# Feed-forward part over two rows at once, with the residual's scaling on ScalarE and the gate on VectorE

## What is computed

```
u  = layernorm(x)                               # over the 256 channels
xh, z = split(u @ W_in)                         # 512 + 512 channels
xc = depthwise conv 3x3 of xh
dt_r, B, C = split(xc @ W_xproj);  dt = softplus(dt_r @ W_dt + b_dt)
h_t = exp(dt_t * A) * h_(t-1) + (dt_t @ W_dtN + b_dtN) * B_t * xc_t      # over 48*48 steps, 512 x 16 states
y_t = sum over states of h_t * C_t + Dskip * xc_t
y  = (layernorm(y) * ln_g + ln_b) * silu(z)     # the gate
x  = x + y @ W_out + b_out                      # the residual
n  = layernorm(x)
out = x + n + two one-hot vectors of 16, times 2 where a token is marked   # "ffn"
```

## Time and profile before

| | us |
|---|---|
| median of 3 runs | 3854.43 (3844.46 to 3861.37) |
| the profiled execution | 3850.34, of which the span from first to last instruction 3848.5 |
| VectorE busy | 3545.4 (92% of the span) |
| POOL, TensorE, ScalarE busy | 3123.7 (81%), 3007.7 (78%), 2946.9 (77%) |
| mean granted TensorE clock | 0.858 of full speed |
| DMA engines | 78.4% of their time, 205 GB/s |

### The profile page before, as it was taken

How to read it: one execution, slowest core, us unless ns; L and a number is a source line. 1 busy time by engine, 2 the same in 40 slices (tenths; PEclk the granted TensorE clock), 3 DMA queues, 4 the chain that set the end, 5 groups by cost and what they waited for, 6 DMA issues and landing times.

```text
span 3848.5 us, 105654 instructions
## 1 busy us (share of the span) xinstructions
PE 3007.7 (78%) x34944; PEld 1624.3 (42%) x34944; DVE 3545.4 (92%) x12174; ACT 2946.9 (77%) x6050; POOL 3123.7 (81%) x5772
## 2 busy tenths in 40 slices
PE   4787888788778887888788878877887788778765
PEld 2344444444444444444444444444444444444332
DVE  2699999999999999999999999999999999999997
ACT  2678777887787778787888787778887888787764
POOL 0688888888888888888888888888888888888885
PEclk7788888888888998888799888988888889988877
DMA  2878887887788878887888778778887888788874
GB/s 60 214 196 216 223 212 201 215 226 205 206 214 220 210 209 211 216 215 209 210 223 215 207 209 223 207 205 208 221 218 205 214 212 222 205 213 217 211 189 105
DMA packets 397438, 790.44 MB, mean 205 GB/s; under 512 B 94553, under 2 KB 249178, under 8 KB 396890
## 3 DMA queue, kind: packets, MB, share of 16 engines
q1 hardware_dynamic: 396890, 783.68, 78.4%
HBM read 648.20 MB, written 96.73 MB: 194 GB/s over the span
## 4 chain that ended last, share of the span: by engine, by line
DVE 43%; ACT 22%; PE 17%; issue 8%; DMA 3%; POOL 3%; SPq 2%; ACTq 0%; POOLq 0%; DVEq 0%
DVE h L910 9%; DVE ps_a L894 7%; ACT ps_a L668 7%; DVE ps_a L897 6%; DVE h L913 6%; PE ps_s L615 4%; PE ps_y L510 3%; ACT ap L678 3%; PE ps_s L577 3%; DVE sz L966 2%; DVE res L1001 2%; ACT y L753 2%; ACT yn L803 2%; PE ps_y L494 2%; ACT xtok L703 2%
## 5 line engine op out<-in xcount | busy, mean ns | idle before, releaser
L668 ACT ACTIVATE ps_a<-dtb,a_n 128x384 f32<-128x384 f32 x2304 | 1252.8, 580 | 387.5 <-DVE h L913 375.7
L1181 POOL TENSOR_TENSOR h<-mp,up 128x128 f32<-128x128 f32 x2304 | 1056.6, 459 | 392.3 <-PE ps_y L510 171.1
L1171 POOL TENSOR_TENSOR mp<-ap,h 128x128 f32<-128x128 f32 x2304 | 1053.9, 457 | 111.3 <-ACT ap L678 0.8
L894 DVE TENSOR_TENSOR ps_a<-ps_a,h 128x192 f32<-128x192 f32 x2304 | 817.4, 355 | 162.1 <-ACT ps_a L668 158.6
L910 DVE SCALAR_TENSOR_TENSOR h<-xb,db,ps_a 128x192 f32<-128x192 f32 x2304 | 923.5, 401 | 7.3 <-PE ps_y L510 4.2
L913 DVE SCALAR_TENSOR_TENSOR h<-xb,db,ps_a 128x192 f32<-128x192 f32 x2304 | 929.7, 404 | 0.0
L510 PE MATMUL ps_y<-h,cw 64*32 64x256 f32 x18432 | 771.3, 453 | 126.1 <-POOL h L1181 75.8
L897 DVE TENSOR_TENSOR ps_a<-ps_a,h 128x192 f32<-128x192 f32 x2304 | 810.0, 352 | 0.0
L678 ACT ACTIVATE ap<-dtb,a_n 128x256 f32<-128x256 f32 x1152 | 521.6, 504 | 154.1 <-POOL h L1181 127.8
L1161 POOL TENSOR_TENSOR up<-xb,db 128x512 f32<-128x512 f32 x576 | 611.5, 1062 | 0.0
L510 PEld LDWEIGHTS ps_y<-h,cw 64*32 64x32 f32 x18432 | 317.1, 120 | 490.4 <-issue 244.0
(11 more groups left out here) (112 smaller groups left out, 4103.7 us busy)
## 6 DMA issues: line engine op xcount, KB each, us to landing
xb<-xd SPq DMA_DIRECT2D x576, 512.0 KB, 7.2
dtb<-xd SPq DMA_DIRECT2D x576, 512.0 KB, 7.0
xs<-xh SPq DMA_DIRECT2D x196, 192.0 KB, 3.6
xd<-dttok SPq DMA_DIRECT2D x288, 128.0 KB, 7.0
xin<-in_x_dram SPq DMA_DIRECT2D x144, 128.0 KB, 4.3
xd<-xtok SPq DMA_DIRECT2D x192, 96.0 KB
res<-in_x_dram SPq DMA_DIRECT2D x144, 128.0 KB, 5.8
out_dram<-res SPq DMA_DIRECT2D x144, 128.0 KB, 2.4
```

The costliest lines, as they stand in the source:

```text
L668: ins = act.activation(ps_a[buf][:, n, 0:2 * VD].rearrange("p (t d) -> p t d", t=2), dtb[:, u % DUNITS, 2 * buf:2 * buf + 2, 0:VD], ACT.Ex ...
L894: dve.tensor_tensor(a[:, 0], a[:, 0], last[:, 0], ALU.mult).then_inc(m0_done, 1)
L1171: pool.tensor_tensor(mp[:, G % 2], ap[:, Q % 2, G % 4], h[:, (G - 1) % HRING, :, VD:HALF], ALU.mult) \
L1181: pool.tensor_tensor(h[:, G % HRING, :, VD:HALF], mp[:, G % 2], up[:, Q % 2, G % 4], ALU.add) \
```

## The change

- The ffn is done for two rows at once, in the second row of each pair: all its tensors get 6 instead of 3 columns of tokens, and rows of even index have no ffn work any more, rows of odd index one set of instructions, twice as wide. All stages stand in place 1, several of them in one slot.
- The residual's scaling goes to ScalarE: six ACTIVATE per pair (`scale_res`).
- `scale_yn` writes back into its PSUM bank, and VectorE multiplies bank by `sz` into `yn` (`gate_y`); the bank is free when that is done.
- The stores wait for the pair, six DMAs at once, and the table `AT` is a new one.

```diff
-    "dttok": (-26, -24, -23), "dtn": (-21,), ... "exp": (-35, -35), "log": (-35, -35),
+    "dttok": (-26, -24, -18), "dtn": (-22,), ... "exp": (-39, -30), "log": (-37, -29),
-    "copy_y": (22, 35, 54), "y_log": (55,), "y_scale": (55,), "y_norm": (62, 63, 64),
+    "copy_y": (22, 35, 53), "y_log": (57,), "y_scale": (59,), "y_norm": (60, 60, 64),
-    "y_stats": (22, 45, 53), "y_shift": (57,), "load_res": (59,), "stack": (-141,),
+    "y_stats": (24, 53, 55), "y_shift": (58,), "load_res": (65,), "stack": (-122,),
-    "cw": (-6, 13, 28), "gate": (68, 69, 70, 71), "store": (103,), "bounce": (-17,), "states": (-5,),
+    "cw": (-9, 1, 37), "gate": (67, 68, 69, 71), "store": (109,), "bounce": (-20,), "states": (-20,),
-    "ffn": (96, 96, 97, 97, 98, 98, 99, 99, 100, 100, 101, 101, 102, 102, 103, 103),
+    "ffn": (99, 99, 101, 101, 102, 102, 102, 103, 103, 103, 104, 104, 106, 106, 106, 107, 107),
+    "res_scale": (101, 102, 102, 104, 104, 105),
...
-        EMPTIED = {..., "yt": yn_ready, ...}
+        EMPTIED = {..., "yt": gated, ...}
...
+            def scale_res(pair, k):
+                if k == 0:
+                    act.wait_ge(ffn, pair * FFN + 2)
+                act.activation(res[:, k, :], res[:, k, :], ACT.Identity, bias=sc2[:, k:k + 1], scale=sc1[:, k:k + 1]) \
+                   .then_inc(res_scaled, 1)
...
             def scale_yn(r, g):
                 act.wait_ge(yt_done, r * NG + g + 1)
-                ...
-                act.activation(yn[:, g, :], shared_bank("yt", r, g)[:, 0:TOK], ACT.Identity, bias=bet[:, g:g + 1],
+                bank = shared_bank("yt", r, g)[:, 0:TOK]
+                act.activation(bank, bank, ACT.Identity, bias=bet[:, g:g + 1], scale=gam[:, g:g + 1]).then_inc(yn_ready, 1)
...
+            def gate_y(r, g):                      # VectorE; POOL's gate_y is gone
+                dve.wait_ge(yn_ready, r * NG + g + 1)
+                dve.wait_ge(sz_ready, r * NG + g + 1)
+                dve.tensor_tensor(yn[:, g, :], shared_bank("yt", r, g)[:, 0:TOK], sz[:, g, :], ALU.mult).then_inc(gated, 1)
...
-                    for k in range(KT):
-                        dve.tensor_scalar(res[:, k, :], res[:, k, :], sc1[:, k:k + 1], sc2[:, k:k + 1],
-                                          ALU.mult, ALU.subtract)
...
                 for r, j in due("ffn", i, s):
-                    if j % 2 == place:
-                        ffn_part(r, j)
+                    if r % 2 == 1 and place == 1:
+                        ffn_part(r // 2, j)
```

More of the change, by code:

```diff
@@ L40 @@
 AT = {
[L41 to L50, removed]
+    "conv": (-48, -46, -45, -44), "xproj": (-43,), "dtp": (-41, -41, -36, -36), "xtok": (-33, -32, -31),
+    "dttok": (-26, -24, -18), "dtn": (-22,), "yt": (66, 67, 68, 69), "out": (76, 79, 80), "z": (33, 34, 36, 37),
+    "xlnT": (-154, -153), "proj": (-149, -148, -146, -145), "exp": (-39, -30), "log": (-37, -29),
+    "copy_y": (22, 35, 53), "y_log": (57,), "y_scale": (59,), "y_norm": (60, 60, 64), "ln1_log": (-171,),
+    "ln1_scale": (-164,), "reload": (41,), "ln2_log": (89,), "ln2_scale": (90,), "ln1_apply": (-158, -158, -154),
+    "y_stats": (24, 53, 55), "y_shift": (58,), "residual": (76, 81, 82), "ln2_stats": (82, 83, 83),
+    "sz": (34, 35, 36, 37), "make_db": (-23,), "ln1_stats": (-180, -177, -175), "ln1_shift": (-161,),
+    "ffn": (99, 99, 101, 101, 102, 102, 102, 103, 103, 103, 104, 104, 106, 106, 106, 107, 107), "dt_add": (-30, -29),
+    "cw": (-9, 1, 37), "gate": (67, 68, 69, 71), "store": (109,), "stack": (-122,), "load_res": (65,),
+    "bounce": (-20,), "states": (-20,), "load_xin": (-181,), "res_scale": (101, 102, 102, 104, 104, 105),
 }
@@ L264, in build @@
         ffn = sem("ffn")
+        res_scaled = sem("res_scaled")
         marked = sem("marked")
@@ L427, in load_residual, with store @@
             def load_residual(r):
-                if r >= 1:
-                    sp.wait_ge(out_stored, r * KT * SEM_DMA)
+                if r >= 2:
+                    sp.wait_ge(out_stored, r // 2 * 2 * KT * SEM_DMA)
                 for k in range(KT):
-                    sp.dma_start(res[:, k, :], row_tokens(x, r, k)).then_inc(res_loaded, SEM_DMA)
-            def store(r):
-                sp.wait_ge(final_ready, r + 1)
-                for k in range(KT):
-                    sp.dma_start(row_tokens(out, r, k), res[:, k, :]).then_inc(out_stored, SEM_DMA)
+                    sp.dma_start(res[:, r % 2 * KT + k, :], row_tokens(x, r, k)).then_inc(res_loaded, SEM_DMA)
+            def store(pair):
+                sp.wait_ge(final_ready, pair + 1)
+                for n in range(2 * KT):
+                    sp.dma_start(row_tokens(out, 2 * pair + n // KT, n % KT), res[:, n, :]).then_inc(out_stored, SEM_DMA)
             load_xin(0)
@@ L878, in _ @@
                         copy_xh(r, j)
-        FFN = 12
         @block.vector
@@ L1062, in between @@
                         y_shift_by(r)
+                    for r, j in due("gate", i, s):
+                        gate_y(r, j)
                     for r, j in due("residual", i, s):
```

176 lines of the change are left out of this document (87 added, 89 removed).

## The result

The changed kernel takes **4168.77 us** (median; 4166.92 to 4178.9), beside 3854.43 us for the kernel before in the same runs (median of three; a fourth was a slow one of 8256.43 us): a ratio of 1.082, 95% interval 1.079 to 1.086. It is 8.2% slower, 314 us over the forecast of 3855 us and 209 us over its upper end.

A forecast was written before the change was run, and what follows sets the result against it. VectorE's work was taken to bound a row (busy 73.3 of 76.7 us), the rest mostly waiting for ScalarE's exp(dt*A). Terms -90 -67 +88 -110 +72 +94 +14 sum to +1: 3855 us on the median's scale, range 3705 to 3960.

The forecast's parts named there:

- Steps 1 to 3: VectorE's own work: residual's scaling leaves -90, ffn for pairs -67, gate arrives +88; 69 us shorter in all.
- Rival D: Back-to-back ffn stages on VectorE each wait for POOL through the port lock: 72 us, 3927 us; chance 0.06.
- Step 4: exp and log spread over slots 9, 11, 18, 19 take back VectorE's waiting around slot 13: -110 us.
- Step 5: Even rows, without ffn in slots 0 to 7, wait for TensorE's conv: +72 us, bounds 0 and 111.
- step 7: y_shift in slot 10 waits for y_scale, and the gate in slots 19 to 23 for ScalarE's scaling: +14 us.
- Step 6: SP stands for the bounce, so dtb for slots 40 to 43 comes late: +94 us, bounds 0 and 212.
- Step 3's other half: Beyond the gate's +88 us on VectorE, nothing was counted for the instructions POOL loses.
- Rival C: SP's wait costs its full bound at dtb for slots 40 to 43: 212 us, 3973 us; chance 0.17.
- A: SP's wait is hidden because the bounce lands quickly in a shorter queue: 3761 us; chance 0.26.

The follow-up runs named there:

- p_only: Changed code with the old slot table and the gate left on POOL (ffn for pairs, scaling on ScalarE): 3836.94 us, ratio 0.997.
- s_only: Kernel before with only the residual's scaling moved to ScalarE, row by row, ffn in every row: 3799.54 us, ratio 0.987.
- s_exp: s_only plus exp at (-39, -36) and log at (-38, -34), spread over slots: 3794.05 us, ratio 0.986.
- p_exp: p_only plus exp at (-39, -36) and log at (-38, -34), spread over slots: 3821.91 us, ratio 0.992.
- s_exp2: s_only plus exp at (-39, -30) and log at (-37, -29), the change's own places: 3831.94 us, ratio 0.996.
- b_stack: Kernel before with one table entry changed, the load of xs (stack) moved from slot 3 to slot 22: 4052.56 us, ratio 1.053.
- a_stack_xin: Changed kernel with stack (-141) and load_xin (-191) put back to their places in the kernel before: 3952.66 us, ratio 1.027.
- a_sp_cw: Changed kernel with stack, bounce, states and cw put back to the slots of before: 4031.88 us, ratio 1.046.
- a_all_pool: a_sx_pool with bounce, states and cw also put back as in the kernel before: 3926.09 us, ratio 1.020.
- g_only: Kernel before with only the gate moved to VectorE, reading y out of its PSUM bank as in the change: 4075.04 us, ratio 1.058.
- g_sb: Kernel before with the gate on VectorE but in SBUF, ScalarE emptying the PSUM bank as before: 3921.33 us, ratio 1.018.
- a_oldtable: Changed code with the old slot table, only the entries of ffn, scaling and store fitted to pairs: 4044.61 us, ratio 1.050.
- a_sx_pool: a_stack_xin with the gate given back to POOL: 3953.01 us, ratio 1.027.
- a_gate_pool: Changed kernel with its new table and the gate given back to POOL: 4172.6 us, ratio 1.083.

## Why the prediction was wrong

Point by point, by its own steps.

- *Steps 1 to 3, VectorE's own work*: -69 forecast, -96 measured. Pairs with scaling give -165 (p_only) for the -157 forecast, the gate +97 for +88; the rest came with the new table. The split was off: scaling alone -61, not -90, and pairs -104, not -67. Rival D's waits between neighbouring stages did not come, rather the reverse: `resi`, whose 1.03 us beside POOL the prediction shows, had a mean of 823 ns before and has 167 in p_only, on twice the columns.

```profile
L1029 DVE TENSOR_TENSOR resi<-dif,shr 128x3 int32<-128x3 f32 x48 | 39.5, 823 | 0.0
```

```profile
L1043 DVE TENSOR_TENSOR resi<-dif,shr 128x6 int32<-128x6 f32 x24 | 4.0, 167 | 0.8
```

- *Step 4*: -110 forecast; slots 12 to 18 lost 128 us of idle. The sum was right, its reason only in part: exp and log spread by themselves won 6 us (s_only to s_exp, too little to tell from none) and 15 us (p_only to p_exp), and at the change's own places lost 32 (s_exp2).
- *Step 5*: +72 forecast. Slots 0 to 11 rose by 120 us over all rows: even rows lose 4.3 us each (103), odd ones 0.75 (18), slot 10 of step 7 included. Right in kind, too small; in p_only each even row lost 5.0, more than row 1's 4.64.
- *Step 6* is the one that failed. Resource right (SP's queue, `dtb`), and the sign. But I asked about one `dtb` only, that for slots 40 to 43, since a new wait stands ahead of it there, and called `load_res` and `stack` a lateness of 1.3 us for that one. The wait for `dtb` is 454 us, not 70 to 120, and stands at slot 31: the load of `xs` moved directly ahead of the `dtb` for slots 32 to 35, which had a lead of 12.5 us for a landing of 8.9. b_stack prices that at 201 us. SP did stand for the bounce as forecast, 9.0 us a row:

```profile
SPq L427 <- DMA bounce<-xp: 431.3, 48, 10.6
```

  But the `dtb` behind it had a mean lead of 8.9 us, not the 5.8 worked out, for a landing of 5.7, and the idle of slots 38 to 47 rose by only 6 us. Once `stack` and `load_xin` are put back (a_stack_xin) it is 51 us of idle more; putting bounce, `states` and `cw` back won 24 us (a_sp_cw) and 27 us (a_all_pool), for the 94 forecast. Step 6 put the cost of the whole queue on its smallest part. `load_xin`, ten slots later, I did not look at; it is 103 us once `stack` is mended.
- *Step 3's other half*: the bank. I priced the gate as own work only and "counted nothing" around it. In the old order the held bank costs 154 us (g_only against g_sb). In the new one neither it nor the gate's own 97 us decide, as VectorE waits anyway. `EMPTIED` is in the description of the kernel, and I did not ask who takes that bank next.
- *Step 7*: 14 forecast. `y_shift`'s slot 10 has 0.45 us a row, 22 us. Small, as said.

Rival C had the sign and the resource ("wait for `dtb` over 200 us") but a bound of 212 us for one place; A and C took their prices from that place. Costs did not add up as a sum, either: code alone is +194 us (a_oldtable), the load of `xs` alone +201, both and the rest together +314, since waits overlap and one mended wait uncovers the next. What stays open is what exactly closes the loop in a_stack_xin and a_sx_pool; the chain names SP and DMA, no run isolates `load_res`. With the gate on POOL in both, the old table takes 3837 us (p_only) and the new one, with `stack`, `load_xin`, `bounce`, `states` and `cw` put back, 3926 (a_all_pool): 89 us lie in the rest of the table, and no run takes them apart.

## What to carry to other kernels

When a table of orders changes, take every DMA that moved and ask which transfer now stands behind it, what lead that one had and what its landing already took: the leads of all twelve `dtb` of a row were in the trace before, and the one that was hit had 12.5 us for a landing of 8.9 and 2 us of exps, 1.6 us to spare. An engine that takes the last read of a shared buffer also takes over when it comes free: find who wants the buffer next before pricing the instruction alone. And VectorE, 92% busy, was the bound only as long as its feeders kept their leads; in the changed kernel saving its work was worth nothing (a_gate_pool, a_sx_pool: 93 and 96 us of work less, 4 and 0 us of time more).

## What was not expected of the hardware

A load of 512 KB whose median landing is 7.0 us took 9.8 us in a stretch where the DMA engines are busy 0.99 of the time, and 11.0 to 11.8 us with 768 KB more issued just ahead; the `xs` loads themselves took 3.6 us in slot 3 and 8.2 to 8.4 us in slot 22. Issue times on SP stretch with it: the median for that `dtb` (rows 3 to 44) is 0.54 us before, 0.77 after and 0.75 in b_stack, though single ones reach 1.7 us before as well. One of b_stack:

```profile
1704.71 1.18 SPq L402 DMA_DIRECT2D dtb<-xd  x1
```
